# Expert rows weighted as they leave their bank and added into the residual in memory

## The reference

```python
# layer 0: x = x + moe(_layernorm(x)); 8 experts, hidden 512, two choices for each row
topw, topi = jax.lax.top_k(probs, K)
topw = topw / (topw.sum(-1, keepdims=True) + 1e-09)
gates = jnp.zeros((T, E), x.dtype).at[jnp.arange(T)[:, None], topi].set(topw)
top_g, tok_idx = jax.lax.top_k(gates.T, cap)            # at most cap = 391 rows an expert
xe = x[tok_idx]
h = jax.nn.silu(xe @ gate_w) * (xe @ up_w)              # (written as einsums)
ye = (h @ down_w) * top_g[..., None]
out = jnp.zeros_like(x).at[tok_idx.reshape(-1)].add(ye.reshape(-1, H))

# layer 1: x = x + moe(_layernorm(x)); 8 experts, hidden 256, softmax over the two best scores
y = jnp.sum(total_probs[..., None] * expert_out, axis=-2)
```

## Time and profile before

| | us |
|---|---|
| three runs | 3393.14, 3391.74, 3396.70 |
| median of the three | 3393.14 |
| the profiled execution: its own time | 3398.03 |
| the profiled execution: span from first to last instruction | 3396.2 |
| PE busy in the span | 3049.8 (90%) |
| DVE busy | 2082.0 (61%) |
| ACT busy | 1259.6 (37%) |
| POOL busy | 407.1 (12%) |
| first expert stage, first product to last bank | about 1150 to 1594 |
| second expert stage | about 3028 to 3331 |

### The profile page before, as it was taken

The page is one execution under the profiler, slowest core; times in us unless marked ns, Lnnn a source line. Parts: engine busy times, 40 slices in busy tenths (PEclk is TensorE's granted clock), DMA queues, the critical chain, the costliest instruction groups (busy, mean ns, idle before and its releaser), DMA issues.

```text
span 3396.2 us, 53242 instructions
## 1 busy us (share of the span) xinstructions
PE 3049.8 (90%) x22228; PEld 2800.3 (82%) x22228; DVE 2082.0 (61%) x3652; ACT 1259.6 (37%) x2163; POOL 407.1 (12%) x302
## 2 busy tenths in 40 slices
PE   6999999899998799997599999989997999969992
PEld 6998896399985588895599997989997999968881
DVE  6985487878777545443766565765274735646664
ACT  4463064344410234332244243443143413335551
POOL 1034433443000100001100000000000000010103
PEclk9999999999998799999699999999998999869996
DMA  7322133131140356535531011452321432248877
GB/s 247 111 55 41 1 87 70 13 85 32 37 117 27 97 177 202 160 131 162 170 111 38 13 41 44 128 129 78 81 87 52 114 86 65 71 146 263 263 250 227
DMA packets 284269, 366.13 MB, mean 108 GB/s; under 512 B 52472, under 2 KB 234782, under 8 KB 282224
## 3 DMA queue, kind: packets, MB, share of 16 engines
q1 hardware_dynamic: 165035, 203.54, 20.2%
q0 software_dynamic: 51248, 68.03, 8.7%
q10 hardware_dynamic: 67717, 90.69, 8.3%
HBM read 285.75 MB, written 83.74 MB: 109 GB/s over the span
## 4 chain that ended last, share of the span: by engine, by line
PE 56%; DVE 5%; DMA 3%; ACT 2%; ACTq 1%; issue 1%; POOL 0%; POOLq 0%; DVEq 0%; SPq 0%
PE PV L463 12%; PE PV L464 12%; PE PV L465 12%; PE PV L567 5%; PE PS L463 3%; PE PS L464 3%; PE PS L465 3%; DMA b<-y_d,gidx 2%; PE PA L598 1%; PE PA L491 1%; DVE b L1850 1%; DVE b_split L1636 1%; PE PA L893 1%; PE PV L884 1%; ACTq L121 1%
## 5 line engine op out<-in xcount | busy, mean ns | idle before, releaser
L463 PE MATMUL PV<-WH,b_split 128*125 128x256 f32 (+2 forms) x3708 | 1092.1, 295 | 123.4 <-DVE b_split L1636 106.6
L464 PE MATMUL PV<-WH,b_split 128*125 128x256 f32 (+2 forms) x3708 | 1078.6, 291 | 0.0
L465 PE MATMUL PV<-WH,b_split 128*125 128x256 f32 (+2 forms) x3708 | 1077.3, 291 | 0.0
L1636 DVE TENSOR_TENSOR b_split<-b,b_split 128x500 fp32r<-128x500 f32 x1040 | 687.8, 677 | 436.6 <-ACT b_split L1252 423.4
L1252 ACT CAST b_split<-b 128x500 fp32r<-128x500 f32 x1040 | 626.0, 613 | 811.5 <-PE PV L465 726.2
L463 PEld LDWEIGHTS PV<-WH,b_split 128*125 128x125 f32 (+2 forms) x3708 | 704.4, 190 | 148.7 <-issue 102.4
L464 PEld LDWEIGHTS PV<-WH,b_split 128*125 128x125 f32 (+2 forms) x3708 | 707.2, 191 | 9.9
L465 PEld LDWEIGHTS PV<-WH,b_split 128*125 128x125 f32 (+2 forms) x3708 | 704.2, 190 | 11.3
L1619 DVE TENSOR_TENSOR WH<-WS,WH 128x1024 fp32r<-128x1024 f32 x292 | 344.5, 1221 | 146.7 <-ACT WH L1237 145.0
L1237 ACT CAST WH<-WS 128x1024 fp32r<-128x1024 f32 x292 | 292.1, 1051 | 178.9 <-PE PV L567 142.2
L463 PE MATMUL PV<-b_split,WH 128*128 128x250 f32 (+3 forms) x1136 | 335.7, 296 | 9.2 <-DVE b_split L1636 6.4
(11 more groups left out here) (270 smaller groups left out, 3617.2 us busy)
## 6 DMA issues: line engine op xcount, KB each, us to landing
WS<-in_L_ffn_w SPq DMA_DIRECT2D x46, 1024.0 KB
WH<-at_d SPq DMA_DIRECT2D x15, 1093.8 KB
WS<-in_L_ffn_gate_w SPq DMA_DIRECT2D x16, 1024.0 KB
WS<-in_L_ffn_up_w SPq DMA_DIRECT2D x16, 1024.0 KB
WS<-in_L_ffn_down_w SPq DMA_DIRECT2D x16, 1024.0 KB
y_d<-b ACTq DMA_DIRECT2D x60, 256.0 KB
y_d<-b ACTq DMA_DIRECT2D x64, 196.0 KB
b<-key_d POOLq DMA_DIRECT2D x4, 2560.0 KB, 9.6
```

The costliest lines, as they stand in the source:

```text
L463: pe.matmul(o, a[0], b[0], start=start, stop=False, **kw)
L464: pe.matmul(o, a[0], b[1], start=False, stop=False, **kw)
L465: return pe.matmul(o, a[1], b[0], start=False, stop=stop, **kw)
L1636: ve.tensor_tensor(lo, src, hi.bitcast(F32), ALU.subtract).then_inc(xl_done, 1)
```

## The change

Weight, residual and addition move:

- `row_tokens` makes two more tables. Row numbers are now counted from 1, so that 0 marks a vacant slot. `tidx` is written first and serves the gathers. `sidx` has for each slot the row to add to, and for a vacant slot a row of its own behind the T real ones (`spare`, an iota on POOL; `x2_d` and the output are longer for it). `wslot` has each slot's weight: DVE builds a matrix (two instructions of 125 x 640 or 125 x 680 elements), PE makes 20 further products with it, in fp32, and DVE copies the bank.
- `store_normed` also writes the residual rows to `acc[layer]`, which is `x2_d` in layer 0 and the output in layer 1 (20 DMAs a layer on ACT's queue).
- Each bank of results is multiplied by its slot's weight as it is copied out, into one of eight tiles of 1024 columns in the residual's place. `y_d` and the stores to it are gone.
- POOL adds each tile to `acc[layer]` by an indirect DMA with an add (`scatter`). Before the first tile of block b it waits until the adds of block b - 1 have landed; the tiles of one block are not ordered. The gather of block b + 3 is issued ahead of the adds of block b. In the blocks behind a branch POOL also waits for that block's adds and for the gather of block b + 3.
- `combine`, its gathers, `store_x2` and the stores of the output are gone. After layer 0, ACT waits for all adds and reads the residual back in five pairs (`x2_back`), for each of which `ln_x2` waits.

```diff
-YRING = (6, 8)
+YRING = 8
...
-        x2_d = dram("x2_d", [T, D])
+        x2_d = dram("x2_d", [T + 4 * P, D])
+        acc = [x2_d, out]
+        wslot, spare = ecnt[:, 0:34], ecnt[:, 40:74]
...
-        y_d = [dram("y0_d", [E * CAPR, D]), dram("y1_d", [BLK * 256, D])]
...
+        def y_number(layer, b, t):
+
+            return b * 4 + t if layer == 0 else E * 4 + b * 2 + t
+
+        def y_tile(layer, n):
+
+            at = (B3, B1)[layer] + n % YRING * D
+            return F[:, at:at + D]
...
+                bank = v.take(pe)
+                pe.wait_ge(weight_hot_ready, layer + 1)
+                for n in range(2 * NT):
+                    mm = pe.matmul(bank[0:r, 0:blocks * tiles], at_row[:, n, :].bitcast(F32),
+                                   at_weight[:, n, :], start=(n == 0), stop=(n == 2 * NT - 1))
+                mm.then_inc(v_full, 1)
+                mark["weights", layer] = v.n
...
-            for i in range(NT):
-                sp.wait_ge(yg_used, 2 * NT + 2 * (i + 1))
-                spread(sp, out[i * R:(i + 1) * R, :], rows(B1)[:, i, :], out_stored)
-            sp.wait_ge(out_stored, BOTH * NT)
...
+                pool.wait_ge(scattered, 16 * GROUPS)
+                if layer == 1:
+                    pool.wait_ge(v_free, mark["weights", 0])
+                pool.iota(spare[:, 0:blocks * tiles], [[0, blocks], [P, tiles]], base=T + 1, channel_multiplier=1,
+                          allow_small_or_imprecise_dtypes=True).then_inc(spare_ready, 1)
+                pool.wait_ge(tidx_ready, layer + 1)
...
+                npiece = tiles * D // HALF
+
+                def scatter(b):
+
+                    for t in range(tiles):
+                        n = y_number(layer, b, t)
+                        for half in range(2):
+                            j = (0 if layer == 0 else E * 8) + b * npiece
+                            j += half * tiles + t if layer == 0 else 2 * t + half
+                            pool.wait_ge((v_free, s_free)[j % 2], y_at[j])
+                        if t == 0 and b:
+                            added(b - 1)
+                        c = b * tiles + t
+                        pool.indirect_dma_start(out=acc[layer],
+                                                out_offset=bass.IndirectOffsetOnAxis(ap=sidx[0:r, c:c + 1], axis=0),
+                                                in_=y_tile(layer, n)[0:r, :], in_offset=None, compute_op=ALU.add)\
+                            .then_inc(y_st[n % YRING], 16)
+
+                def added(b):
+                    for t in range(tiles):
+                        n = y_number(layer, b, t)
+                        pool.wait_ge(y_st[n % YRING], 16 * (n // YRING + 1))
+
+                def landed(b):
+                    if b < blocks:
+                        pool.wait_ge(xe_full[b % 2], 16 * (4 * 4 * layer + tiles * (b // 2 + 1)))
...
-                for b in range(min(FIXED[layer] + 1, blocks)):
-                    gather(b)
-                for b in range(FIXED[layer] + 1, blocks):
-                    with pool.If(used > b - 1):
-                        gather(b)
-
-                pool.wait_ge(route_ready, layer + 1)
-                if layer == 1:
-                    pool.wait_ge(y_filled, 16 * NFILL)
-                def results_stored(pieces):
-                    for q in range(4):
-                        pool.wait_ge(y_st[q], 16 * pieces // 4)
-
-                results_stored(E * 8 + layer * FIXED[1] * 4)
+                gather(0)
+                gather(1)
+                pool.wait_ge(acc_init[layer], BOTH * NT)
+                pool.wait_ge(v_free, mark["weights", layer] - 1)
+                gather(2)
+                for b in range(FIXED[layer]):
+                    if b + 3 < blocks:
+                        gather(b + 3)
+                    scatter(b)
+                added(FIXED[layer] - 1)
+                landed(FIXED[layer] + 1)
+                landed(FIXED[layer] + 2)
                 for b in range(FIXED[layer], blocks):
                     with pool.If(used > b):
-                        results_stored(E * 8 + (b + 1) * 4)
-                for n in range(2 * NT):
-                    i, k = divmod(n, 2)
-                    if n >= YRING[layer]:
-                        pool.wait_ge(yg_used, 2 * NT * layer + n - YRING[layer] + 1)
-                    pool.indirect_dma_start(out=y_slot(layer, n), out_offset=None, in_=y_d[layer],
-                                            in_offset=bass.IndirectOffsetOnAxis(ap=gidx[0:R, k, i:i + 1], axis=0))\
-                        .then_inc(yg_full[layer][n % YRING[layer]], 16)
+                        if b + 3 < blocks:
+                            gather(b + 3)
+                        scatter(b)
+                        added(b)
+                        landed(b + 3)
...
+                    spread(act, acc[layer][i * R:(i + 1) * R, :], rows((B3, B1)[layer])[:, i, :], acc_init[layer])
...
-                        if j >= 4:
-                            act.wait_ge(y_st[j % 4], 16 * (j // 4))
-                        act.copy(ffn_y(layer, j % 4)[0:r, :], s.read(act)[0:r, :]).then_inc(s_free, 1)
-                        for jj, pp, done in ((j - 1, p - 1, v_free), (j, p, s_free)):
-                            nd, t = divmod(pp, tiles) if layer == 0 else (pp % 2, pp // 2)
-                            act.wait_ge(done, y_at[jj])
-                            act.dma_start(y_d[layer][(b * tiles + t) * r:(b * tiles + t + 1) * r,
-                                                     nd * HALF:(nd + 1) * HALF],
-                                          ffn_y(layer, jj % 4)[0:r, :]).then_inc(y_st[jj % 4], 16)
+                        half, t = divmod(p, tiles) if layer == 0 else (p % 2, p // 2)
+                        n, c = y_number(layer, b, t), b * tiles + t
+                        if n >= YRING:
+                            act.wait_ge(y_st[n % YRING], 16 * (n // YRING))
+                        act.activation(y_tile(layer, n)[0:r, half * HALF:(half + 1) * HALF], s.read(act)[0:r, :],
+                                       ACT.Copy, scale=wslot[0:r, c:c + 1]).then_inc(s_free, 1)
...
-            def store_x2(j):
-
-                g = j - NPIECE
-                if not 0 <= g < NB:
-                    return
-                act.wait_ge(yg_used, 4 * (g + 1))
-                spread(act, x2_d[2 * g * R:2 * (g + 1) * R, :].rearrange("(t p) d -> p t d", p=R),
-                       rows(B3)[:, 2 * g:2 * g + 2, :], x2_stored)
+            for q in range(YRING):
+                act.wait_ge(y_st[q], 16 * (E * 4 // YRING))
+            for g in range(NB):
+                spread(act, rows(B3)[:, 2 * g:2 * g + 2, :],
+                       x2_d[2 * g * R:2 * (g + 1) * R, :].rearrange("(t p) d -> p t d", p=R), x2_back[g])
...
-                emptied(ve.tensor_copy(tidx[0:r, 0:w], v.read(ve)[0:r, 0:w]))
+                bank = v.read(ve)[0:r, 0:w]
+                vacant = rbf[0:r, 448:448 + w]
+                ve.tensor_scalar(tidx[0:r, 0:w], bank, -1.0, 0.0, ALU.add, ALU.max).then_inc(tidx_ready, 1)
+                ve.wait_ge(spare_ready, layer + 1)
+                d(ve.scalar_tensor_tensor(out=vacant, in0=bank, scalar=0.0, in1=spare[0:r, 0:w],
+                                          op0=ALU.is_equal, op1=ALU.mult))
+                d(ve.tensor_tensor(at_weight, past[:, :, 0:w], past[:, :, 1:], ALU.subtract))
+                d.sync()
+                ve.tensor_tensor(at_weight, at_weight,
+                                 wide(wk[0:R, :, :].rearrange("p k i -> p (k i)"), w), ALU.mult)\
+                    .then_inc(weight_hot_ready, 1)
+                d(ve.scalar_tensor_tensor(out=vacant, in0=vacant, scalar=-1.0, in1=bank, op0=ALU.add, op1=ALU.add))
+                d.sync()
+                emptied(ve.tensor_copy(sidx[0:r, 0:w], vacant))
+                ve.tensor_copy(wslot[0:r, 0:w], v.read(ve)[0:r, 0:w]).then_inc(v_free, 1)
...
-                                ve.wait_ge(y_st[j % 4], 16 * (j // 4))
-                            emptied(ve.tensor_copy(ffn_y(layer, j % 4)[0:r, :], v.read(ve)[0:r, :]))
+                            half, t = divmod(p, tiles) if layer == 0 else (p % 2, p // 2)
+                            n, c = y_number(layer, b, t), b * tiles + t
+                            if n >= YRING:
+                                ve.wait_ge(y_st[n % YRING], 16 * (n // YRING))
+                            emptied(ve.tensor_scalar(y_tile(layer, n)[0:r, half * HALF:(half + 1) * HALF],
+                                                     v.read(ve)[0:r, :], wslot[0:r, c:c + 1], None, ALU.mult))
...
-            def combine(layer, res, g):
-
-                for n in range(4 * g, 4 * g + 4):
-                    i, k = divmod(n, 2)
-                    ve.wait_ge(yg_full[layer][n % YRING[layer]], 16 * (n // YRING[layer] + 1))
-                    if k:
-                        ve.wait_ge(yg_used, 2 * NT * layer + n)
```

(8 more changed lines are left out.)

69 lines of the change are left out of this document (26 added, 43 removed).

## The result

| | before | after |
|---|---|---|
| median, us | 3394.6 (3391.74 to 3396.7, 4 runs) | 3312.8 (3307.75 to 3313.23, 4 runs) |
| ratio | 1 | 0.976, 95% interval 0.974 to 0.978 |
| profiled execution, us (its span) | 3398.0 (3396.2) | 3312.9 (3311.2) |

The change takes 85 us from the span and 82 from the median.

What follows compares the result with a forecast made beforehand. PE was taken to bound the expert stages, and combination the two stretches behind them. Terms -56 - 25 + 1 + 8 = -72 us gave 3326 us for the profiled execution and 3321 for the median, range 3300 to 3364.

Steps and rivals of the forecast that it cites:

- PE's share in the first stage: Sign in the first expert stage: PE busy for less than 0.97 of it would make the prediction wrong in kind.
- the length of the second: Sign in the second expert stage: 303 to 312 us long, with DMA share near 0.95.
- The pairs "every 10 us": Sign behind the first expert stage: the pairs of the next projection's lead come every 10 us.
- The end: End of the program: only the last add follows ACT's last copy, 8 us to the end; -56 us, bounds -60 and -45.
- The boundary: Behind the first expert stage: combinations go, a readback of the sums comes in; -25 us, bounds -10 and -30.
- The starts: Ahead of each expert stage: new DVE work and 20 fp32 products, hidden in layer 0; +1 us, bounds 0 and +13.
- The stores: Residual-row stores added on ACT's queue, other stores' issues removed: 0 to -3 us, taken as 0.
- Inside the stages: Adds replace stores; in layer 1 some weight loads come late, half a microsecond a block: +8 us, bounds 0 and +35.
- X: Engine time of one 4 KB row add in place of a store: taken as 0.40 us, between 0.20 and 0.48.
- Late weights: Rival, chance 0.22: DMA demand of 1.03 stretches the second stage from 303 to 347 us, +44 in place of +8; 3357.
- The slower case: Rival, chance 0.05: adds take far longer than two moves and pace layer 1; at 1.0 us an add, 3447.
- The part on the gathers: POOL's gathers inside the stages: rows are needed 40 us later, so an add of under 30 us costs nothing.

Runs made afterwards that it cites:

- The kernel without that tail: Kernel before, without the gathers and combinations behind the second expert stage, output stored as the residual stands: 3338.6 us, ratio 0.984.
- the doubled adds: Changed kernel with every indirect add issued a second time, into a scratch table that nothing reads: 3412.1 us, ratio 1.005.
- the kernel with the added writes: Changed kernel with the same rows also written once beside each add, without adding, into a scratch table: 3348.5 us, ratio 0.987.

## Why the prediction was right, and where its sizes were off

Its mechanism is what the profile shows: the gain is the two stretches behind the stages, 84 of 85 us, and the stages did not pay. Of its signs, the end (11.5 us behind the copy), the first LayerNorm (17.3), the start (+2.0), PE's share in the first stage (435.9 of 441.0 us) and the length of the second (303.3) hold. The pairs "every 10 us" hold in the mean only: they come 4.9, 9.3, 12.9 and 14.1 us apart.

**The end** (-56): the profile has -53.6. The step gave 8 us from last copy to end and it took 11.5. With a write in place of the add it is 7.8 us: the step under-priced the add's landing, not the path. The kernel without that tail gains 55, so the term is shown.

**The boundary** (-25): -30.6. The step took 21 us for the combinations of four pairs, 6 for the earlier start, and gave 2 back to TensorE. The start gave 4.6: the last add landed 10.5 us behind the last copy, where 8 were taken, and the readback took 6.2, where 7.3 were. From first LayerNorm to sixth evacuation it went from 98.9 to 72.9 us, 26.0. In that stretch stood the combinations of the four later pairs, 16 x 1.286 = 20.6, as the step had it. The other 5.4 are where it gave 2 back. TensorE's granted clock did not stay low; these windows, before and after, have nearly the same number of products:

```profile
1615.60:1714.50 98.90, 60.13 (x388) 57.14 (x389) 65.73 (x102) 29.45 (x56) 15.81 (x11) 0.74 0.60 190
```

```profile
1608.90:1681.80 72.90, 52.48 (x381) 50.72 (x382) 45.62 (x85) 29.38 (x56) 0.00 (x0) 0.83 0.54 154
```

PE was 60.1 us busy with them at a mean granted clock of 0.74, and 52.5 us at 0.83. That the 5.4 us come from there is a reading of two traces; no run separates it.

**The starts** (+1): +2.0 in the second stage. The step took 7 us for the 40 records and they took 8.7; with that its sum gives 2.5 us and not 0.8, and 2.0 was measured. The mechanism, the split behind the copy, was named; the kernel that undoes it gets 1.4 of the 2.0 back, and the rest goes with the 40 records, which hold TensorE when the rows land.

**The stores** (0): no run takes them apart; both stages are as long as before.

**Inside the stages** (+8): +0.6, the term that was most mis-sized. Its first half was nearly right: X was taken as 0.40 us and came out 0.37 by queues (0.32 net), the share as 0.97 and came out 0.93 in the window. The rule of the Trainium skill named there (Collectives: The Full Stack, the bandwidth ceiling) gave an estimated 0.39, from the second source read. The traces come near it: an add held an engine 2.2 times as long as a write of the same row, by these means, where the page has 1.93. The page measured collectives; the second read itself shows in no trace here. The second half, about 0.5 us a block for late weights, did not come: there was one wait of 0.9 us, as before. A share of 0.93 in a window did not make the loads late. The experiments show that the mean share doesn't decide alone: the kernel with the gather behind the adds has late loads at 0.83, because of when its bursts fall, and the changed kernel has next to none at 0.90. What more work does was shown: 302 us of engine time in place of 273 make the stage 17.5 us longer, 339 make it 57.

**The rivals.** Late weights is a real mechanism: it is what the doubled adds and the gather behind the adds bring on. It was put at a higher X (0.48) and misses the measured X by 0.11. The slower case put its break-even at X = 0.78. Two adds a row, 0.65 to 0.74 us of an engine, gave 1.005 of the time before already: the second stage grew by 57 us, under the 80 of that sum, but the first stage, the boundary and the end grew by 39 more, which the rival put at nothing. What no rival and no term held is that the order of gather and add is worth 21 us. The part on the gathers asked only whether the rows come in time, and would have given the kernel with the gather behind the adds the same time. That the changed kernel has the better order was luck, as far as the prediction goes.

The sum: the terms miss by +2.4, -5.6, +1.0 and -7.4 us, and 3.4 us more (-2.4 in the first stage, -2.6 elsewhere, +1.6 at the first start) lie within what two runs of one kernel differ by. That makes 13 us against the profiled execution, 85 and not 72. The median misses by 8 only, since the forecast took off 4.9 for the distance of profile and median before, and after the change there is none; that is luck. One bound is added up wrongly: with the upper bounds of its own terms (-45, -10, +13, +35) the forecast reaches 3386, not 3335. The measured time lies far from there.

## What to carry to other kernels

Adding into memory by transfer pays where it takes a serial stretch away, and it was free in a stage whose engines it took from 0.77 to 0.90 busy. Count demand from prices of a row, here 2.2 writes for an add, and not from bytes, and take the result as an upper estimate: the prices gave 39 and 89 us of engine time where the runs showed 29 and 66. Below that limit look at when bursts fall. Here the gather, which had room to wait, went ahead of the adds, and the two didn't meet in front of a load with a deadline; put behind them, at the same bytes, it cost 12 us in the second stage. And when work is left out to price it, count the blocks first: the run without adding looked 24 us faster, and a block that other routing had saved is worth 20.

## What the runs showed of the hardware

- An indirect add of a row of 4 KB from on-chip memory into HBM held a DMA engine 0.37 us in the changed kernel's second stage, a plain indirect write 0.165, a gather 0.20. The price falls when there are more: the second adds of the doubled kernel brought 0.28 us a row, the second writes 0.12. An add's issue takes POOL 1.55 us where a gather's takes 1.0.
- An add of 128 rows has landed about 9 us after its issue in the stage (8.8 us median in the window); adds of 98 rows, waited for one by one behind the first stage, went at one in 6.1 us.
- The 16 engines were 0.94 busy over 321 and 361 us with the loads late; the most seen in 100 us was 0.98, in the kernel with the added writes.
- The same transfers, issued in 6 us with the adds first and not in 8 us with the gathers first, made blocks of 20.0 us up to 2.0 us longer, 12 us over the stage, with the engines 0.83 busy and not 0.89.
- 20 exact fp32 products (125 x 128 by 34 columns) ran as 40 records in 8.7 us.
